# Splitting the row scan of a four-stage network into two streams of two pictures

## The reference, cut to what matters

```python
def _L1_conv_ref(fea, W, b):
    kh = W.shape[2]
    Wm = W[:, :, (kh - 1) // 2, 0]
    bb = b[None, :, None]

    def step(carry, x):
        new = jax.nn.relu(jnp.einsum('oc,ncw->now', Wm, carry) + bb) + x
        return (new, new)
    xs = jnp.moveaxis(fea, 2, 0)
    _, ys = jax.lax.scan(step, xs[0], xs[1:])
    down = jnp.concatenate([xs[:1], ys], axis=0)
    _, ys2 = jax.lax.scan(step, down[-1], down[:-1], reverse=True)
    stack = jnp.concatenate([ys2, down[-1:]], axis=0)
    return jnp.moveaxis(stack, 0, 2)
...
x = x + _L1_conv_ref(_ln_c(x), L1_conv_W, L1_conv_b)
```

## Time and profile before

| | |
|---|---|
| runs of the kernel | 1055.58, 1052.45, 1054.76 us; median 1054.76 |
| profiled execution | 1055.37 us, its span 1053.8 us |
| mean granted TensorE clock | 0.954 of full speed |
| TensorE busy | 945.8 us, 90% |
| VectorE busy | 673.9 us, 64% |
| ScalarE busy | 518.2 us, 49% |
| scan, from the first product to the last row's first half | 873.99 to 940.92 us |

### The profile page before, as it was taken

The page is one execution under the profiler, slowest core; times in us unless marked ns, Lnnn a source line. Parts: engine busy times, 40 slices in busy tenths (PEclk is TensorE's granted clock), DMA queues, the critical chain, the costliest instruction groups (busy, mean ns, idle before and its releaser), DMA issues. The chain is left out here.

```text
span 1053.8 us, 21102 instructions
## 1 busy us (share of the span) xinstructions
PE 945.8 (90%) x7764; PEld 622.4 (59%) x7765; DVE 673.9 (64%) x1276; ACT 518.2 (49%) x834; POOL 151.4 (14%) x167
## 2 busy tenths in 40 slices
PE   5977489899999999999999999999999949975796
PEld 4434444367676666766667766767674428862453
DVE  5378887555666555566556665665675876668773
ACT  3722544435565455555446565655663303233674
POOL 0030001300121011011102210221114820002000
PEclk9998579989999999999999999999999979996998
DMA  8700045446877666686766886776888520000001
GB/s 293 266 0 1 0 144 194 141 159 211 256 230 254 205 208 210 213 256 203 233 212 210 269 262 202 218 255 213 252 217 266 156 78 1 1 0 1 1 21 60
DMA packets 162114, 173.11 MB, mean 164 GB/s; under 512 B 54273, under 2 KB 132097, under 8 KB 162082
## 3 DMA queue, kind: packets, MB, share of 16 engines
q1 hardware_dynamic: 149570, 138.70, 41.0%
q0 software_dynamic: 9808, 32.12, 9.7%
q10 hardware_dynamic: 2704, 1.87, 0.5%
HBM read 146.44 MB, written 14.68 MB: 153 GB/s over the span
## 5 line engine op out<-in xcount | busy, mean ns | idle before, releaser
L964 DVE SCALAR_TENSOR_TENSOR w_lo<-raw,w_hi 128x1024 f16<-128x1024 f32 x144 | 172.3, 1222 | 75.0 <-ACT w_hi L883 75.0
L1096 PE MATMUL gate_ps<-x,w_hi 128*128 128x256 f16 (+2 forms) x576 | 172.2, 299 | 13.1 <-DVE w_lo L964 5.8
L1097 PE MATMUL gate_ps<-x,w_hi 128*128 128x256 f16 (+2 forms) x576 | 172.0, 299 | 0.0
L1098 PE MATMUL gate_ps<-x,w_lo 128*128 128x256 f16 (+2 forms) x576 | 171.9, 298 | 0.0
L1096 PE MATMUL up_ps<-x,w_hi 128*128 128x256 f16 (+2 forms) x576 | 171.3, 297 | 0.0
L1097 PE MATMUL up_ps<-x,w_hi 128*128 128x256 f16 (+2 forms) x576 | 171.2, 297 | 0.0
L1098 PE MATMUL up_ps<-x,w_lo 128*128 128x256 f16 (+2 forms) x576 | 171.1, 297 | 0.0
L883 ACT ACTIVATE w_hi<-raw 128x1024 f16<-128x1024 f32 x144 | 147.6, 1049 | 8.0 <-SPq L785 5.5
L889 ACT CAST h_hi<-hid 128x320 f16<-128x320 f32 (+1 forms) x144 | 68.5, 476 | 154.1 <-DVE hid L969 154.1
L964 DVE SCALAR_TENSOR_TENSOR w_lo<-raw_last,w_hi 128x1024 f16<-128x1024 f32 x72 | 88.2, 1225 | 74.9 <-ACT w_hi L883 74.9
L972 DVE TENSOR_TENSOR h_lo<-hid,h_hi 128x320 f16<-128x320 f32 (+1 forms) x144 | 74.1, 515 | 78.1 <-ACT h_hi L889 78.1
(11 more groups left out here) (256 smaller groups left out, 1446.9 us busy)
## 6 DMA issues: line engine op xcount, KB each, us to landing
raw<-in_gate_up SPq DMA_DIRECT2D x96, 512.0 KB, 4.5
raw_last<-in_gate_up SPq DMA_DIRECT2D x32, 512.0 KB, 4.2
raw<-in_down SPq DMA_DIRECT2D x32, 512.0 KB, 4.4
raw_last<-in_down SPq DMA_DIRECT2D x32, 512.0 KB, 3.7
weights<-in_f SPq DMA_DIRECT2D x3, 2816.0 KB, 16.3
slot_y<-y_sb POOLq DMA_DIRECT2D x16, 512.0 KB, 3.2
raw<-in_sgate SPq DMA_DIRECT2D x6, 512.0 KB, 6.4
raw<-in_sup SPq DMA_DIRECT2D x6, 512.0 KB, 7.7
```

What stands on the lines that cost most here:

```text
L964: V.scalar_tensor_tensor(w_lo[:, j % RING, c], raw[j % RING][:, c], W_SCALE, w_hi[:, j % RING, c], ALU.mult, ALU.subtract).then_inc(split_ ...
L1096: T.matmul(out, hi_a, hi_b, start=first, stop=False, **flags)
L1097: T.matmul(out, hi_a, lo_b, start=False, stop=False, **flags)
L1098: return T.matmul(out, lo_a, hi_b, start=False, stop=last, **flags)
```

## The change

The four pictures are split in two streams, q = 0 with pictures 0 and 1, q = 1 with 2 and 3, of `STREAM` = 32 columns each. A step does all of its work for stream 0 and then for stream 1, on every engine. Each stream has its own part of row_hi, row_hi_low and row_lo, its own PSUM bank for each parity (all four output tiles of 32 columns lie in one), and its own semaphores. TensorE has 8 bias matmuls and 48 products a stream, of 32 columns, so 112 a step where 56 were. VectorE has three operations a stream (row_hi, state, row_lo, one after the other, each over all four channel tiles of two pictures) and ScalarE one, so six and two a step as before, and each of as many numbers as before. VectorE's row_hi no longer waits for `hi_low_made`.

```diff
 SIDE = BATCH * IMW
+STREAM = SIDE // 2
...
-        row_hi = sb("row_hi", [P, KC, SIDE], F16)
-        row_hi_low = sb("row_hi_low", [P, KC, SIDE], F16)
-        row_lo = sb("row_lo", [P, KC, SIDE], F16)
+
+        ones_row = sb("ones_row", [1, STREAM], F16)
+        low_row = sb("low_row", [1, STREAM], F16)
+        row_hi = sb("row_hi", [P, 2, KC, STREAM], F16)
+        row_hi_low = sb("row_hi_low", [P, 2, KC, STREAM], F16)
+        row_lo = sb("row_lo", [P, 2, KC, STREAM], F16)
...
-        stepped = sem("stepped")
-        hi_made = sem("hi_made")
-        hi_low_made = sem("hi_low_made")
-        lo_made = sem("lo_made")
-        added = sem("row_added")
+        stepped = [sem(f"stepped{q}") for q in range(2)]
+        hi_made = [sem(f"hi_made{q}") for q in range(2)]
+        hi_low_made = [sem(f"hi_low_made{q}") for q in range(2)]
+        lo_made = [sem(f"lo_made{q}") for q in range(2)]
+        added = [sem(f"row_added{q}") for q in range(2)]
...
             def low(s):
-                for g in range(2):
-                    k = slice(2 * g, 2 * g + 2)
-                    act.wait_ge(hi_made, 2 * s + g + 3)
+                for q in range(2):
+                    act.wait_ge(hi_made[q], s + 2)
                     act.nop(nofuse=True)
-                    S.mul(row_hi_low[:, k, :], row_hi[:, k, :], 1.0 / LOW_SCALE).then_inc(hi_low_made, 1)
+                    S.mul(row_hi_low[:, q, :, :], row_hi[:, q, :, :], 1.0 / LOW_SCALE).then_inc(hi_low_made[q], 1)
 
...
             def one(s, new, parity):
-                def out(m):
-                    return step_ps[parity][m // 2][:, (m % 2) * SIDE:(m % 2 + 1) * SIDE]
-
-                def products(weights, row, k, m, **flags):
-                    return T.matmul(out(m), weights[:, k, m * P:(m + 1) * P], row[:, k, :], skip_group_check=True,
-                                    start=False, **flags)
-
-                pe.wait_ge(added, 2 * s + 1)
-                for m in range(KC):
-
-                    T.matmul(out(m), bias_hi[:, m * P:(m + 1) * P], ones_row[:, :], start=(m % 2 == 0), stop=False,
-                             skip_group_check=True)
-                    T.matmul(out(m), bias_lo[:, m * P:(m + 1) * P], low_row[:, :], start=False, stop=False,
-                             skip_group_check=True)
-
-                for g in range(2):
-                    pe.wait_ge(hi_made, 2 * s + g + 1)
-                    for k in (2 * g, 2 * g + 1):
-                        for m in range(KC):
-                            products(conv_hi, row_hi, k, m, stop=False)
-                for g in range(2):
-                    pe.wait_ge(hi_low_made, 2 * s + g + 1)
-                    for k in (2 * g, 2 * g + 1):
-                        for m in range(KC):
-                            products(conv_lo, row_hi_low, k, m, stop=False)
-                pe.wait_ge(lo_made, 2 * s + 1)
-                for k in (0, 1):
+                for q in range(2):
+                    def out(m):
+                        return step_ps[parity][q][:, m * STREAM:(m + 1) * STREAM]
+
+                    def products(weights, row, last=False):
+                        for k in range(KC):
+                            for m in range(KC):
+                                mm = T.matmul(out(m), weights[:, k, m * P:(m + 1) * P], row[:, q, k, :],
+                                              skip_group_check=True, start=False, stop=last and k == KC - 1)
+                        return mm
+
+                    pe.wait_ge(added[q], s + 1)
                     for m in range(KC):
-                        products(conv_hi, row_lo, k, m, stop=False)
-                pe.wait_ge(lo_made, 2 * s + 2)
-                for g in range(2):
-                    for m in (2 * g, 2 * g + 1):
-                        for k in (2, 3):
-                            mm = products(conv_hi, row_lo, k, m, stop=(k == 3))
-                    mm.then_inc(stepped, 1)
+                        T.matmul(out(m), bias_hi[:, m * P:(m + 1) * P], ones_row[:, :], start=(m == 0), stop=False,
+                                 skip_group_check=True)
+                        T.matmul(out(m), bias_lo[:, m * P:(m + 1) * P], low_row[:, :], start=False, stop=False,
+                                 skip_group_check=True)
+                    pe.wait_ge(hi_made[q], s + 1)
+                    products(conv_hi, row_hi)
+                    pe.wait_ge(hi_low_made[q], s + 1)
+                    products(conv_lo, row_hi_low)
+                    pe.wait_ge(lo_made[q], s + 1)
+                    products(conv_hi, row_lo, last=True).then_inc(stepped[q], 1)
 
...
-            dve.sem_inc(added, 3)
+            for q in range(2):
+                dve.sem_inc(added[q], 2)
...
+            def row_of(new, q):
+                n = slice(2 * q, 2 * q + 2)
+                return state[:, new, :, n, :].rearrange("p k n w -> p k (n w)") if isinstance(new, int) else \
+                    state[:, bass.ds(new, 1), :, n, :].rearrange("p o k n w -> p (o k) (n w)")
+
+            for q in range(2):
+                V.tensor_copy(row_hi[:, q, :, :], row_of(0, q)).then_inc(hi_made[q], 1)
+                dve.wait_ge(hi_made[q], 1)
+                V.tensor_tensor(row_lo[:, q, :, :], row_of(0, q), row_hi[:, q, :, :], ALU.subtract).then_inc(lo_made[q], 1)
 
             def one(s, new, parity):
-                def add(g, out):
-                    k, row = chunks(new, g)
-                    return V.scalar_tensor_tensor(out if out is not None else row,
-                                                  step_ps[parity][g][:, 0:2 * SIDE].rearrange("p (k c) -> p k c", k=2),
-                                                  0.0, row, ALU.max, ALU.add)
-
-                for g in range(2):
-                    k, row = chunks(new, g)
-                    dve.wait_ge(stepped, 2 * s + g + 1)
-                    dve.wait_ge(hi_low_made, 2 * s + g + 1)
+                for q in range(2):
+                    def add(out):
+                        return V.scalar_tensor_tensor(out, step_ps[parity][q][:, 0:KC * STREAM].rearrange("p (k c) -> p k c", k=KC),
+                                                      0.0, row_of(new, q), ALU.max, ALU.add)
+
+                    dve.wait_ge(stepped[q], s + 1)
                     dve.nop(nofuse=True)
-                    add(g, row_hi[:, k, :]).then_inc(hi_made, 1)
-                for g in range(2):
-                    k, row = chunks(new, g)
-                    dve.wait_ge(hi_made, 2 * s + 4)
+                    add(row_hi[:, q, :, :]).then_inc(hi_made[q], 1)
+                    dve.wait_ge(hi_made[q], s + 2)
                     dve.nop(nofuse=True)
-                    add(g, None).then_inc(added, 1)
-                for g in range(2):
-                    k, row = chunks(new, g)
-                    dve.wait_ge(added, 2 * s + g + 4)
+                    add(row_of(new, q)).then_inc(added[q], 1)
+                    dve.wait_ge(added[q], s + 3)
                     dve.nop(nofuse=True)
-                    V.tensor_tensor(row_lo[:, k, :], row, row_hi[:, k, :], ALU.subtract).then_inc(lo_made, 1)
+                    V.tensor_tensor(row_lo[:, q, :, :], row_of(new, q), row_hi[:, q, :, :],
+                                    ALU.subtract).then_inc(lo_made[q], 1)
 
```

More of the change, by code:

```diff
@@ L1220, in scan @@
         mv, rstd = keep["scan_mv"], keep["scan_rstd"]
-        ones_row = sb("ones_row", [1, SIDE], F16)
-        low_row = sb("low_row", [1, SIDE], F16)
-        row_hi = sb("row_hi", [P, KC, SIDE], F16)
-        row_hi_low = sb("row_hi_low", [P, KC, SIDE], F16)
-        row_lo = sb("row_lo", [P, KC, SIDE], F16)
+        ones_row = sb("ones_row", [1, STREAM], F16)
[3 more added lines that the diff above has]
+        row_lo = sb("row_lo", [P, 2, KC, STREAM], F16)
         xc = sb("xc", [P, NT, C])
@@ L1339, in _ @@
             dve.wait_ge(state_ready, NT)
-            def chunks(new, g):
-                k = slice(2 * g, 2 * g + 2)
-                row = state[:, new, k, :, :].rearrange("p k n w -> p k (n w)") if isinstance(new, int) else \
-                    state[:, bass.ds(new, 1), k, :, :].rearrange("p o k n w -> p (o k) (n w)")
-                return k, row
-            for g in range(2):
-                k, row = chunks(0, g)
-                V.tensor_copy(row_hi[:, k, :], row).then_inc(hi_made, 1)
-                dve.wait_ge(hi_made, g + 1)
-                V.tensor_tensor(row_lo[:, k, :], row, row_hi[:, k, :], ALU.subtract).then_inc(lo_made, 1)
```

## The result

The changed kernel takes 1084.4 us, the median of four runs (1080.2 to 1085.9); the kernel before takes 1054.5, the median of four. The ratio is **1.028, with a 95% interval of 1.025 to 1.031**. The forecast was 1086, in a range of 1077 to 1098.

What follows compares the result with a forecast made beforehand. TensorE was to bound the changed scan: 2.91 us of issue plus 0.36 of shape changes, 3.27 us a step instead of 2.24. With the ends, 30.9 us more on 1055.4 gave 1086 us, range 1077 to 1098.

Steps and rivals of the forecast that it cites:

- The bound: In the scan's step after the change, TensorE's 3.27 us exceeds VectorE's 2.20 us, so TensorE sets the pace.
- The step that carried the sign: TensorE's 0.6 us of standing a step goes; 1.3 us of issue and 0.36 us of shape changes replace it.
- TensorE's standing: TensorE's waiting in a step of the kernel before, 0.6 us of 2.24; the change was to remove it.
- the passages: TensorE's changes between 128-row products and one-row bias matmuls, either way: 0.09 us each, four a step, 0.36 us.
- The pair: One weight load with its 32-column matmul on TensorE: 26 ns from start to start, 112 a step, 2.91 us.
- The first rival: A load with its product stays at 29 ns whatever the columns: 1097 us, 1098 with loop heads; chance 0.27.
- the third: A load with its product falls with its columns to 15.7 ns, VectorE sets the pace: 1054 us; chance 0.08.
- VectorE's slack: VectorE's dependent operations take 1.10 us a stream, 2.20 us a step, under TensorE's 3.27 us.
- loop heads: The gap where a loop's round begins, 0.13 us above a shape change: costed at nothing, 1.6 us if uncovered.
- tail: End of the scan, after the last row_hi: one VectorE chain of 1.08 us; 0.5 us gained on the old tail.
- The fourth rival: The granted clock falls from 1.00 in the scan, with 0.50 as the router's example: some 1184 us; chance 0.03.

Runs made afterwards that it cites:

- the run with half a load: Changed kernel with products whose weights are 64 of the 128 columns of an output tile, half of the sums left out; 1167.3 us in one execution.

## Why the prediction was right

*The bound.* The step that carried the sign held: 112 pairs a step cost more than TensorE's standing saves. TensorE does not wait, the extra VectorE operation is free, and a term taken from TensorE (the passages, the second biases) comes back one for one.

*The pair.* Forecast 26 ns, between 15.7 and 29.1; it is 25.0. The bounds from rows could not place it; 26, "near the upper end", was a guess that came close, and here luck had a part. The Trainium skill's floor of about 25 ns was exact, and by it the forecast would have been 1083. The first rival (29 ns whatever the columns) and the third (columns alone) both fall.

*The passages.* Forecast 0.09 us each, four a step; they are 0.083 and 0.079, and the way back, which no row had shown, costs as much. Each of them also costs some 14 ns at the second matmul behind it. (The kernel before has this too: of the seven distances read as 31 ns for a bias pair, the first is 39 and the others are 29 to 30.) In sum 112 x 0.025 = 2.80, 0.32 and 0.06 make 3.18 us a step, where 3.27 was forecast: 30 x 0.09 = 2.7 us of the 3.0 by which the copy starts earlier than forecast (970.7 for 973.7).

*VectorE's slack, loop heads, tail.* As forecast: a turn of 1.59 us hides a chain of 1.08; each of the 59 passages to the biases is 108 ns, at a loop's head or not; the tail is 1.38 us.

*What was wrong.* The fourth rival's price. I doubled every pair for half the clock and came to 1184 us. At 0.50 the pair takes 27 ns instead of 25, so the floor of 25 ns does not double with the cycle; that the load needs the 27 is inferred from the run with half a load. The doubling was read from the router's products, and it does not carry over to every shape: 40 ns for 25 with 48 columns. The rival looks likelier than its 0.03 for such code: one execution with extra VectorE work and, by their mean clocks, three with written-out loops had it, while the changed kernel's own four have 0.952 to 0.956. It was worth 30 x 0.25 = 7.5 us at most. And "TensorE's standing, 2.24 - 1.62 = 0.6 us a step, does go" was right but hid the cheaper way: in the kernel before 0.4 us of it went with the loops written out and without the empty waits.

## What to carry to other kernels

Splitting a serial chain into streams can pay only if the work of a stream shrinks with its size; a weight load with a matmul stopped shrinking at 25 ns, here somewhere between 64 columns (29 ns) and 48 (25 ns), so halving 64 columns took TensorE's issue from 1.62 to 2.80 us a step. No run here shows a split that pays. Before splitting, price the chain's links themselves: loops with register waits and empty waiting instructions were worth some 12 us together, and taking them away changes no data. Going between 128-row matmuls and a group of one-row ones cost 0.08 us each way where TensorE was the bound; zeros in the other 127 rows are cheaper.

## What the runs showed of the hardware that was not expected

- The granted clock can be 0.50 while TensorE issues without a pause: all but the first microseconds of the scan with 16 columns, more than 30 us with 32 columns in one execution, all but the first two microseconds with 64-column weights. Why it fell there and not in the changed kernel stays open. The changed kernel's profiled scan has 1.00, and so has every other experiment with full products but for a step or the stretch shown. What it costs depends on the pair: 27 ns for 25 with 32 columns, 40 for 25 with 48.
- At 0.50 a pair takes 27 ns with 16 and with 32 columns, and 54 ns with 64 instead of 128 columns of weights. At 1.00 narrower weights are slower too, 32 ns for 25.
- Written out, the same 30 steps need 9% to 13% less time a step (2.00 us for 2.21 and 2.29) where a chain through two engines is the bound, and no less where TensorE is (3.18 us both times).
